# Five places for a projection's split operands, quantiser steps laid by VectorE's free time, and four banks for the sums of the second batch

## The reference, cut to what matters

```
x = x + attention(layernorm(x), ctx) @ wo        # 32 query heads, 8 key/value heads, 128 wide, rotary positions
x = x + router(layernorm(x))                     # 64 experts, top 8 of a softmax: flat * w_sum + w_dense @ expert_bias
x = x + fake_quant(layernorm(x)) @ fake_quant(ctx)   # 8 bit codes, (1024 x 1024) per batch
x = x + (silu(x @ dq(w1).T) * (x @ dq(w2).T)) @ dq(w3).T   # hidden width 2752
```

## Time and profile before

| | us |
|---|---|
| median of three runs | 3135.76 |
| the profiled execution | 3126.09 |
| its span in the trace | 3124.3 |
| PE busy | 2937.6 (94%) |
| DVE busy | 2282.7 (73%) |
| ACT busy | 1926.9 (62%) |
| POOL busy | 1125.5 (36%) |

### The profile page before, as it was taken

The page is one execution under the profiler, slowest core; times in us unless marked ns, Lnnn a source line. Parts: engine busy times, 40 slices in busy tenths (PEclk is TensorE's granted clock), DMA queues, the critical chain, the costliest instruction groups (busy, mean ns, idle before and its releaser), DMA issues. The chain is left out here.

```text
span 3124.3 us, 39400 instructions
## 1 busy us (share of the span) xinstructions
PE 2937.6 (94%) x14144; PEld 2398.6 (77%) x14144; DVE 2282.7 (73%) x3330; ACT 1926.9 (62%) x2627; POOL 1125.5 (36%) x670
## 2 busy tenths in 40 slices
PE   7999999998999999999999888989998988999899
PEld 6878788886888888888888666767876777777787
DVE  5878778786888888888888445876566777777733
ACT  4665766565888888888888586544332555555511
POOL 5728268886333333332332455343000211111100
PEclk9999999999999999999999999999999999999999
DMA  5455334444222222222221677435554542222211
GB/s 181 140 181 167 136 125 135 145 137 167 75 78 85 89 82 81 92 82 79 88 88 54 239 264 269 163 128 192 205 184 166 202 155 69 74 81 81 68 34 57
DMA packets 231489, 399.89 MB, mean 128 GB/s; under 512 B 19840, under 2 KB 106880, under 8 KB 229248
## 3 DMA queue, kind: packets, MB, share of 16 engines
q1 hardware_dynamic: 225792, 372.22, 35.3%
q0 software_dynamic: 5504, 25.17, 2.3%
HBM read 279.48 MB, written 117.83 MB: 127 GB/s over the span
## 5 line engine op out<-in xcount | busy, mean ns | idle before, releaser
L1114 DVE CUSTOM_DVE_ANT_0 at_sc<-at_s,at_mk 128x1024 f32<-128x1024 f32 x256 | 311.9, 1219 | 105.5 <-issue 104.3
L1129 DVE TENSOR_TENSOR at_ptl<-at_t,at_pth 128x512 fp32r<-128x512 f32 x512 | 326.7, 679 | 32.6 <-ACT at_pth L1076 32.1
L1076 ACT ACTIVATE at_pth<-at_t 128x512 fp32r<-128x512 f32 x512 | 276.8, 594 | 96.0 <-PE at_t L1176 95.6
L1066 ACT ACTIVATE at_pr<-at_sc,at_low 128x1024 f32<-128x1024 f32 x256 | 295.5, 1154 | 64.9 <-DVE at_low L1114 35.7
L133 PE MATMUL fr_acc<-fr_xh,fr_wh 128*128 128x512 f32 x768 | 300.2, 391 | 7.6 <-POOL fr_wl L720 5.9
L135 PE MATMUL fr_acc<-fr_xh,fr_wl 128*128 128x512 f32 x768 | 299.3, 390 | 0.0
L134 PE MATMUL fr_acc<-fr_xl,fr_wh 128*128 128x512 f32 x768 | 299.3, 390 | 0.0
L1176 PE MATMUL at_t<-ident,at_pr 128*128 128x128 f32 x2048 | 269.2, 274 | 25.0 <-DVE at_ptl L1129 23.9
L1176 PEld LDWEIGHTS at_t<-ident,at_pr 128*128 128x128 f32 x2048 | 235.2, 140 | 70.8 <-issue 36.5
L242 ACT ACTIVATE fr_nf_above<-fr_nf_raw,sharp 128x1024 f32<-128x1024 f32 (+1 forms) x196 | 215.8, 1102 | 112.5 <-DVE fr_nf_val L268 52.3
L133 PE MATMUL tl_pa<-tl_ring_h 128*128 128x512 f32 x512 | 212.1, 414 | 46.0 <-POOL tl_ring_l L1972 32.3
(11 more groups left out here) (229 smaller groups left out, 7889.1 us busy)
## 6 DMA issues: line engine op xcount, KB each, us to landing
tl_ring<-o_d SPq DMA_DIRECT2D x128, 256.0 KB, 3.4
tl_ring<-in_L_xattn_wo SPq DMA_DIRECT2D x128, 256.0 KB, 4.0
tl_raw<-dq SPq DMA_DIRECT2D x63, 512.0 KB, 3.8
fr_raw<-in_L_xattn_wq SPq DMA_DIRECT2D x32, 512.0 KB, 4.7
q_d<-fr_res SPq DMA_DIRECT2D x64, 256.0 KB, 2.4
rows<-q_d SPq DMA_DIRECT2D x64, 256.0 KB, 2.7
at_inv_row<-r_d SPq DMA_DIRECT2D x64, 256.0 KB, 3.5
o_d<-at_ot SPq DMA_DIRECT2D x64, 256.0 KB, 2.0
```

The lines of the kernel that those rows point to most:

```text
L1066: act.activation(pr[:, n % 2], sc[:, n % 2], ACT.Exp, bias=low[:, n % 2:n % 2 + 1], scale=-1.0, accum_out=sums[:, h % 2, quarter:quarter + ...
L1076: act.activation(pt[0][:, h % 2, j * HALF:(j + 1) * HALF, (n % QT) * P:(n % QT + 1) * P], t_ps[:, j], ACT.Copy).then_inc(t_hi.sem, 1)
L1114: dve.tensor_tensor_reduce(sc[:, n % 2], s_ps[:, n % 2], mk[:, bb * QT + n % QT], -1.0, -NEG, ALU.add, ALU.min, low[:, n % 2:n % 2 + 1]).t ...
L1129: dve.tensor_tensor(pt[1][sl], t_ps[:, j], f32(pt[0][sl]), ALU.subtract).then_inc(t_lo.sem, 1)
```

## The change

The high and low rings get a fifth place, and the engines fill them three slots ahead. To make room, `xT` and `qaT` lie in `rows`, the buffer of the context passes. The first weights are loaded at slot 118 (FIRST - 10) and not 104, and SP first waits for the last store of the first chain's units, since the buffers now overlap. `Spread` takes a cost for each step in place of one for all, and the second chain's weight of a slot is an estimate of what DVE has free in it. From item 16 on (slot 220) DVE does the quantiser's steps before the low parts of hidden values and weights. The down tiles of pairs 3 to 6, computed while batch 1 is alone, rotate through all four banks of `pa`.

```diff
+VECTOR_COSTS = [2.3 if j == AHEAD else 1.0 if j <= NP4 else 2.0 if j == NS4 - 1 else 0.4 for j in range(NS4)]
...
+        spent_by = list(itertools.accumulate(costs[k % NS4] for k in range(total)))
...
-            edge.append(int(total * run / whole + 1e-6))
+            edge.append(sum(s <= spent_by[-1] * run / whole + 1e-6 for s in spent_by))
...
-    SWEEPS, RING = 2 * B, 4
+    SWEEPS, RING = 2 * B, 5
...
-            xT = sb_first("xT", [P, DC, P], F32)
-            qaT = sb_first("qaT", [P, 2, DC, P], BF16)
...
-            ring_h = sb_first("ring_h", [P, 4, 2, 512], F32R)
-            ring_l = sb_first("ring_l", [P, 4, 2, 512], F32R)
+            ring_h = sb_first("ring_h", [P, plan.RING, 2, 512], F32R)
+            ring_l = sb_first("ring_l", [P, plan.RING, 2, 512], F32R)
+
+        xT = rows[:, 0].rearrange("p (c n) -> p c n", c=DC)
+        qaT = rows[:, 1].bitcast(BF16).rearrange("p (s c n) -> p s c n", s=2, c=DC)
...
-            return 1.0 if s[0] == "gate" else 0.3
+            busy = 1.3 if s[0] == "down" else 0.7 * (len(plan.turns.get(q - 1, [])) + 2 * len(plan.gates_done(q - 1, 1)))
+            return max(2.7 + 0.4 * len(plan.turns.get(q, [])) - busy, 0.3)
+
+        F2 = plan.item_slot[2 * plan.EARLY]
...
+        RING, LEAD = plan.RING, plan.RING - 2
...
+        WIDE = range(plan.y_base[plan.EARLY // 2 - 1], plan.y_base[plan.EARLY - 1])
+
+        def y_bank(d):
+            return d % 4 if d in WIDE else 2 + d % 2
+
+        def y_freed(d):
+
+            users = [e + 1 for e in range(max(d - 4, 0), d) if y_bank(e) == y_bank(d)]
+            return users[-1] if users else 0
...
+                        sp.wait_ge(nf1.stored[s], 16 * (1 + sum(len(u[1]) for u in o_units[s::2])))
...
-                if q == FIRST - 24:
+                if q == FIRST - 10:
...
-                if q >= 4:
-                    act.wait_ge(heads, q - 3)
-                act.activation(ring_h[:, q % 4], ring[:, q % 4], ACT.Copy).then_inc(ring_hi, 1)
+                if q >= RING:
+                    act.wait_ge(heads, q - RING + 1)
+                act.activation(ring_h[:, q % RING], ring[:, q % 4], ACT.Copy).then_inc(ring_hi, 1)
...
-                if q + 2 < FIRST:
-                    high(q + 2)
+                if q + LEAD < FIRST:
+                    high(q + LEAD)
...
-                for i, xx in plan.turns.get(q - 1, []):
+                for i, xx in plan.turns.get(q - 1, []) if q <= F2 else []:
                     weight_low(i, xx)
-                for i, j in plan.gates_done(q - 1, 1):
+                for i, j in plan.gates_done(q - 1, 1) if q <= F2 else []:
                     hidden_low(i, j)
...
+                for i, j in plan.gates_done(q - 1, 1) if q > F2 else []:
+                    hidden_low(i, j)
+                for i, xx in plan.turns.get(q - 1, []) if q > F2 else []:
+                    weight_low(i, xx)
...
+                    if i == 2 * plan.EARLY and j == 0:
+                        pe.wait_ge(added, max(d for d in WIDE if y_bank(d) == u) + 1)
...
-                if d >= 2:
-                    pe.wait_ge(added, d - 1)
+                if y_freed(d):
+                    pe.wait_ge(added, y_freed(d))
+                elif d in WIDE:
+                    pe.wait_ge(gone, plan.a_no[plan.EARLY - 1, 0] + 1)
                 else:
                     pe.wait_ge(o_added, 4 * QT)
```

More of the change, by code:

```diff
@@ L13 @@
+import itertools
 import math
@@ L298, with __init__ @@
 class Spread:
-    def __init__(self, units, weights, lag=1, sync_lag=1, ahead=AHEAD, norm_lag=1):
+    def __init__(self, units, weights, lag=1, sync_lag=1, ahead=AHEAD, norm_lag=1, costs=(1.0,) * NS4):
         total = units * NS4
         edge, run, whole = [0], 0.0, float(sum(weights))
+        spent_by = list(itertools.accumulate(costs[k % NS4] for k in range(total)))
         for w in weights:
             run += w
-            edge.append(int(total * run / whole + 1e-6))
+            edge.append(sum(s <= spent_by[-1] * run / whole + 1e-6 for s in spent_by))
         edge[-1] = total
@@ L1511, in weight2 @@
                 return 0.0
-            return 1.0 if s[0] == "gate" else 0.3
+            busy = 1.3 if s[0] == "down" else 0.7 * (len(plan.turns.get(q - 1, [])) + 2 * len(plan.gates_done(q - 1, 1)))
+            return max(2.7 + 0.4 * len(plan.turns.get(q, [])) - busy, 0.3)
+        F2 = plan.item_slot[2 * plan.EARLY]
         spread1 = Spread(len(o_units), [weight1(q) for q in range(FIRST)], lag=1, sync_lag=2)
-        spread2 = Spread(len(f_units), [weight2(q) for q in range(TOTAL)], lag=1, sync_lag=2)
+        spread2 = Spread(len(f_units), [weight2(q) for q in range(TOTAL)], lag=1, sync_lag=2, costs=VECTOR_COSTS)
         parts1, parts2 = ([sum(len(us[v][0]) for v in range(u % 2, u, 2)) for u in range(len(us))]
@@ L1762, in link @@
                                    pc[:, chain.no[key] % 2].rearrange("p (c n) -> p c n", c=4), ACT.Copy).then_inc(c_act, 1)
-            for q in range(2):
+            for q in range(LEAD):
                 high(q)
             for q in range(TOTAL + 2):
-                if q + 2 < FIRST:
-                    high(q + 2)
+                if q + LEAD < FIRST:
+                    high(q + LEAD)
                 for n in range(NC):
@@ L1799, in low @@
                 dve.wait_ge(ring_hi, q + 1)
-                dve.tensor_tensor(ring_l[:, q % 4], ring[:, q % 4], f32(ring_h[:, q % 4]), ALU.subtract).then_inc(ring_lo_d, 1)
+                dve.tensor_tensor(ring_l[:, q % RING], ring[:, q % 4], f32(ring_h[:, q % RING]), ALU.subtract).then_inc(ring_lo_d, 1)
             def add_heads(w):
@@ L1833, in add @@
                 dve.wait_ge(y_tiles, d + 1)
-                dve.tensor_tensor(X[sl], pa[:, 2 + d % 2], X[sl], ALU.add).then_inc(added, 1)
+                dve.tensor_tensor(X[sl], pa[:, y_bank(d)], X[sl], ALU.add).then_inc(added, 1)
             def link(kind, b, t, h):
@@ L1946, in _ @@
                     add_heads(w)
-                if q + 2 < FIRST and q % 2:
-                    low(q + 2)
+                if q + LEAD < FIRST and (q + LEAD) % 2:
+                    low(q + LEAD)
                 for i, j in plan.gates_done(q - 1, 1):
@@ L1971, in low @@
                 pool.wait_ge(ring_hi, q + 1)
-                pool.tensor_tensor(ring_l[:, q % 4], ring[:, q % 4], f32(ring_h[:, q % 4]), ALU.subtract).then_inc(ring_lo_p, 1)
+                pool.tensor_tensor(ring_l[:, q % RING], ring[:, q % 4], f32(ring_h[:, q % RING]), ALU.subtract).then_inc(ring_lo_p, 1)
             def clip_context(n):
@@ L2004, in _ @@
             low(0)
+            low(2)
             for q in range(TOTAL + 2):
-                if q + 2 < FIRST and q % 2 == 0:
-                    low(q + 2)
+                if q + LEAD < FIRST and (q + LEAD) % 2 == 0:
+                    low(q + LEAD)
                 if q == 3:
@@ L2035, in project @@
                 q = w * HQ + h
-                r = q % 4
+                r = q % RING
                 pe.wait_ge(ring_lo_d if q % 2 else ring_lo_p, q // 2 + 1)
@@ L2084, in down @@
                 for s in range(2):
-                    last = split_matmul(pe, pa[:, 2 + d % 2], [hT[:, e, s, t * P:(t + 1) * P] for e in range(2)],
+                    last = split_matmul(pe, pa[:, y_bank(d)], [hT[:, e, s, t * P:(t + 1) * P] for e in range(2)],
                                         [dn[s][:, e, n * 512:(n + 1) * 512] for e in range(2)], s == 0, s == 1)
```

## The result

The changed kernel took 3098.69 us (median of four runs, 3097.48 to 3100.92) where the kernel before took 3136.8 beside it: a ratio of 0.9881 (95% interval 0.9868 to 0.9893). Measured once more on another chip it was 0.989 (0.9871 to 0.9909). The forecast was 3098 us. Its total was right; of its parts, the four banks were right, the fifth place with the moved loads was nearly absent (some 3 us where 14 were forecast), and steps and order brought half as much again as forecast (26 and not 17).

A forecast was written before the change was run, and what follows sets the result against it. TensorE was taken as the bound of the last stage, busy 368 of 405 us where both batches run. Gains of 4 + 4 + 6 + 7 + 14 + 3 = 38 us took the median 3135.8 to 3098 us, range 3078 to 3131.

The forecast's parts named there:

- TensorE is the bound, and its stops and their tails are what can be won: Last stage: TensorE busy 368 of 405 us with both batches; about thirty stops, each tail priced at 1.7 us.
- Steps and order, 14 net: Stretch with both batches, 2549 to 2954 us: 21 us gained from bank waits and tails, less charges, 14 net.
- the 2 for the new order: Stretch with both batches: a net charge of 2 us for doing quantiser steps before the weights' low halves.
- Rival (d): Both batches: low halves behind the steps come late and stop TensorE; slower, 3167 us; chance 0.07.
- The last unit's end, 3: Stop at 2963 us, 8 with its tail: step 6 comes one slot earlier, 3 us gained.
- Four banks, 7: Second batch alone, 2413 to 2549 us: bank waits and tails of 7.5 us, of which 7 gained.
- The fifth place, 4 + 4: Projection: splits one slot earlier; 4 us between heads 14 and 50, 4 us at two later stops behind POOL.
- the 10 that was named as a sign: Projection: TensorE's waits for POOL's split should be under 10 us behind the start.
- The load's move, 6: First weight loads, slot 104 to 118: 7 of a stop's 9 us gained, 1 charged, net 6 us.
- rival (c): Projection: the loads stop TensorE at slot 118 as they did at 108; 3106 us; chance 0.08.
- (a): Whole last stage: the stops only move; 16 us left, so 3120 us; chance 0.27.
- (b): VectorE's idle time is really filled and the lag at the groups disappears; 70 us, so 3066; chance 0.10.

The follow-up runs named there:

- e6_order: The kernel before with the low parts behind the quantiser's steps from slot 221 on, the steps laid as before: 3110.51 us, ratio 0.9932.
- e5_steps: The kernel before with the quantiser's steps laid by VectorE's free time, the low parts left in front of them: 3117.62 us, ratio 0.9956.
- e3_banks: The kernel before with four banks for the sums of pairs 3 to 6 alone: 3124.32 us, ratio 0.9977.
- e1_ring: The kernel before with the fifth place of the high and low rings, its buffer layout and the first weight loads at slot 118: 3130.46 us, ratio 0.9989.
- e2_move: The kernel before with the first weight loads at slot 118 in place of 104, nothing else: 3131.18 us, ratio 0.9992.
- e10_ring_low2: The kernel before with the fifth place and loads at slot 118, but VectorE's split of odd heads kept two ahead: 3113.51 us, ratio 0.9943.
- e4: The kernel before with the steps laid by VectorE's free time and the low parts behind them, no ring, no banks: 3106.11 us, ratio 0.9917.
- e7: The changed kernel without the fifth place and its layout, with the weight loads back at slot 104: 3100.99 us, ratio 0.9903.
- e9: The changed kernel with VectorE's split of odd heads back at two heads ahead: 3079.79 us, ratio 0.9839.
- e11: e9 with five places for the raw operands too: 3075.61 us, ratio 0.9821.
- e12: e9 with VectorE's new order from slot 129 on: 3068.97 us, ratio 0.9794.

## Why the prediction was right, and where it was not

- *TensorE is the bound, and its stops and their tails are what can be won.* Right. Of the 24.6 us of slots 220 to 335, 12.4 are bank waits and 9.6 are PE's busy time for the same matmuls, the tails. The sum had 13.8 and 7 for them. In the five other kernels with this code the tails gave back 4 to 7 us less.
- *Steps and order, 14 net.* Mis-sized, and for a wrong reason. The gross gain of 21 came out as 24.6 in the changed kernel and as 18 to 21 in the five others with this code; the charges did not come: 5 us of new stops inside the groups can't be seen (the whole sum of bank waits is 15.9, near the 14 named), and the 2 for the new order had the wrong sign (by the profile of e6_order it is worth 15.6 us in these slots). The prediction gave the direct gain to where the steps are laid. e5_steps shows that the laying alone leaves the bank waits at 27.8 us, and e6_order that the order alone halves them and is worth 21 us. The row with the answer stood in the earlier trace rows: VectorE idle for 37.7 us behind ScalarE's high half, on the engine that PE waits for. I had listed it as an argument, and priced it inside a charge of 2. Rival (d), low halves too late, had its mechanism (8.9 us of such waits in e6_order) at a fraction of its price. With both parts together they are 4.9. (By the prediction's own prices this rival would have decided from 12 stops on, not 11.)
- *The last unit's end, 3.* Under-sized: 8.1 us in slots 336 to 339, where each edit alone also shortens them (e5 4.1, e6 6.1). The stop of 6.60 us is gone whole, and its tail.
- *Four banks, 7.* Right: 7.2 us by e3_banks, and the waits fell from 5.0 to 1.1 us. In the profile slots 176 to 219 are only 3 to 5 us below those of e1, e2 and e6, so the size rests on the timed runs (4 to 11 us by their interval).
- *The fifth place, 4 + 4.* It failed as a mechanism. The pace stayed (3.49 us per head and 3.47), but not for the reason given, that a deeper ring cannot make such a stretch faster: with VectorE's split left in its place it fell to 3.38, and with five raw places too to 3.19. Two stops behind POOL did shrink; the waits for POOL's split behind the start are 10.9 us, just over the 10 that was named as a sign. What the prediction left out is that LEAD 3 is odd: it moves VectorE's split from odd to even slots, in front of other operations of the chain, and behind a copy that waits for VectorE itself. "No instruction is added; each split is issued one slot earlier" was true and not enough; what the split stands in front of had to be listed. With the move it is worth 3 us by e1_ring, perhaps nothing, and without VectorE's part of it 18 (e10_ring_low2), so the bound of some 20 that I named from the waits was nearer than the pace row I chose.
- *The load's move, 6.* Over-sized: 2.5 us by its ratio, with an interval that includes zero, and 3.3 in the profiled slots 108 to 110. I gave the three loads 7 of the 9 us of the stop; without them 4.08 of its 7.42 us remained. In the changed kernel it is 1.85, with 4.5 us in the slot behind, and nothing is left of the move's gain there (slots 108 to 110: 20.8 and 20.3 us). No stop came at slots 118 to 122, so rival (c) is out; the SP issue behind the moved loads took 1.84 us. The prediction weighed a rule there, the Trainium skill's "DMA: Bandwidth & Descriptors", section "Queues, rings and completion order": descriptors are consumed in ring order on each DMA engine. I had worked out from it that the move lightens nothing. The timed 2.5 us, with an interval that includes zero, cannot be told from that, but the profile speaks against it: slots 108 to 110 became 3.3 us shorter and slots 118 to 122 no longer.
- *Rivals and signs.* (a), only moved stops, holds for the projection and not for the rest. (b), VectorE's idle time really filled, is the true mechanism of the feed-forward part; its 70 us needed the ring's 14 and the load's and banks' 16 as well. Steps and order measured 26 us by e4 and the banks 7, and 3 for ring and move: 36, against 34 to 38 for the whole. The forecast's 38 was 17 (14 and 3), 7 and 14. So the total was met because an error of 9 us in one part and of 11 in another cancelled.

Left open: slots 220 to 335 took 374.2 and 374.5 us in the two executions of the changed kernel and 378.1 to 380.8 in e4, e7, e9, e11 and e12, which have the same code there. Most of the 4 us lies in single slots behind stops (243, 251 or 315, and 323), and there in the granted clock. In slot 323 the stop before is equally long in all of them; in slot 243 it is 1.6 us in the two and 2.0 in the others. Why the clock fell behind a stop in the one and not behind the same stop in the other, the traces do not show.

## What to carry to other kernels

On an in-order engine, look first for its own waits, not only for who waits for it: an operation that isn't ready and stands in front of ready work costs that work its time, and to put it behind was worth more (21 us) than to lay the same work out more evenly (14). Do it only where there is ready work: at the kernel's end the same edit put one operation that wasn't ready before one that was, and cost 2.7 us. When a buffer gets another place and the work goes one slot further ahead, write down for each engine what the moved operation now stands in front of; the parity of an alternation between two engines can turn a gain of 18 us into 3. And a right total proves no term: only the parts run alone showed which of them earned it.

## What the runs showed of the hardware

Three things that I had not expected. PE's busy time for the same 1634 matmuls was 362.1 us at a mean granted clock of 0.96 and 352.6 at 0.99, so two fifths of what was won in that stretch was clock given back and stands in no wait. Equal stops are not followed by equal clocks: behind stops of 2.35 and 2.36 us at one place the granted clock was 1.00 in one kernel and 0.62 in the other, and the slot took 2.9 or 4.4 us, so one profiled execution is not read more finely than this. And the SP queue's issue behind the codes took 0.58 us without the three weight loads before it and 6.25 with them, so 1.5 MB more in front made it ten times as long. That repeats: 6.05 to 6.58 us in the six traces with the loads at 104, and 0.58 or 0.59 in the eight with them at 118. PE's stop at that place was 4.08 us without the loads (e2_move) and 7.42 with them.
